# Attention and a routed feed-forward on one core: where the 15 one-tile units stand in the order of 75, and how the last unit is added

## The reference

```
x = x + attention(layernorm(x), ctx, ctx)        # 16 heads of 16, four projections with biases
n = layernorm(x)
p = softmax(n @ router)                          # 8 experts; the best 2 of each token, their
w = softmax(top_2(p))                            # probabilities softmaxed once more
x = x + sum over the 2 experts e: w_e * ((silu(n @ gating_e) * (n @ up_e)) @ down_e)
```

## Time and profile before

| | |
|---|---|
| median of 3 executions | 1276.99 us (1273.31 to 1278.37) |
| the profiled execution: its time | 1274.27 us |
| its span in the trace | 1272.5 us |
| PE busy | 1221.5 us, 96% of the span |
| PE weight loads | 991.1 us, 78% |
| DVE busy | 645.8 us, 51% |
| ACT busy | 561.3 us, 44% |
| POOL busy | 424.4 us, 33% |
| mean granted clock of PE | 0.991 of full speed |

### The profile page before, as it was taken

How to read it: one execution, slowest core, us unless ns; L and a number is a source line. 1 busy time by engine, 2 the same in 40 slices (tenths; PEclk the granted TensorE clock), 3 DMA queues, 4 the chain that set the end, 5 groups by cost and what they waited for, 6 DMA issues and landing times.

```text
span 1272.5 us, 30742 instructions
## 1 busy us (share of the span) xinstructions
PE 1221.5 (96%) x11214; PEld 991.1 (78%) x11215; DVE 645.8 (51%) x1762; ACT 561.3 (44%) x924; POOL 424.4 (33%) x354
## 2 busy tenths in 40 slices
PE   6999999999999999799999999999999999999996
PEld 3677777777767676578887888888888888888996
DVE  3778888888888778623453222332222222232332
ACT  3566666666666665535322222222222322222442
POOL 3211333333333333322464222223332322222322
PEclk9999999999999999899999999999999999999999
DMA  4444455545545332424344333333333433333332
GB/s 130 138 117 122 152 152 149 157 151 154 155 140 151 114 117 82 106 48 67 77 89 71 50 50 50 53 52 53 50 50 50 54 50 52 51 50 43 53 51 33
DMA packets 171586, 112.44 MB, mean 88 GB/s; under 512 B 103345, under 2 KB 158641, under 8 KB 171473
## 3 DMA queue, kind: packets, MB, share of 16 engines
q1 hardware_dynamic: 143984, 72.75, 23.2%
q0 software_dynamic: 26400, 37.09, 16.6%
q10 hardware_dynamic: 1088, 1.05, 0.3%
HBM read 48.59 MB, written 45.46 MB: 74 GB/s over the span
## 4 chain that ended last, share of the span: by engine, by line
PE 89%; DVE 4%; DMA 2%; issue 2%; ACT 1%; SPq 0%; POOL 0%; another core or an unknown queue 0%; ACTq 0%; POOLq 0%; DVEq 0%
PE banks L522 71%; PE banks L551 5%; PE banks L565 4%; PE banks L576 4%; DVE row_max L1028 1%; PE banks L528 1%; PE banks L557 1%; DMA heads<-qT 1%; PE banks L592 1%; DMA out<-x_sb,token 1%; PE banks L600 1%; DVE att_rows L1041 1%; DVE q_less L1035 1%; DMA ctxT_sb<-in_ctx 0%; PE banks L606 0%
## 5 line engine op out<-in xcount | busy, mean ns | idle before, releaser
L481 POOL DMA_INDIRECT out<-x_sb,token x135 | 210.4, 1559 | 478.2 <-DVE x_sb L1346 413.5
L873 ACT ACTIVATE qT<-banks 128x1024 f32<-128x1024 f32 (+1 forms) x75 | 70.4, 939 | 488.6 <-PE banks L522 430.4
L1333 DVE TENSOR_TENSOR heads<-qT,banks 128x1024 f32<-128x1024 f32 (+1 forms) x75 | 83.5, 1113 | 356.7 <-PE banks L522 338.8
L522 PE MATMUL banks<-xnT,probs 128*128 128x256 f32 (+1 forms) x1184 | 242.7, 361 | 4.4 <-issue 4.4
L522 PE MATMUL banks<-down_sb,heads 128*128 x1080 | 245.5, 379 | 1.2 <-DVE x_sb L1346 0.9
L522 PE MATMUL banks<-xnT,kT 128*128 128x256 f32 (+1 forms) x1216 | 244.8, 359 | 0.0
L522 PEld LDWEIGHTS banks<-xnT,probs 128*128 128x128 f32 x1184 | 208.6, 191 | 32.9 <-issue 7.9
L522 PEld LDWEIGHTS banks<-xnT,kT 128*128 128x128 f32 x1216 | 213.1, 192 | 26.6 <-issue 1.0
L522 PEld LDWEIGHTS banks<-down_sb,heads 128*128 128x128 f32 x1080 | 204.0, 190 | 29.2 <-issue 2.2
L434 POOL DMA_INDIRECT sorted_x<-xn,slots_now x128 | 125.2, 978 | 251.5 <-PE banks L551 139.6
L1028 DVE TENSOR_REDUCE row_max<-banks 128x16 f32<-128x2048 f32 x64 | 146.6, 2291 | 64.2 <-PE banks L551 64.1
(11 more groups left out here) (165 smaller groups left out, 1269.2 us busy)
## 6 DMA issues: line engine op xcount, KB each, us to landing
xn<-sorted_x SPq DMA_DIRECT2D x240, 64.0 KB
x_sb<-in_x SPq DMA_DIRECT2D x16, 512.0 KB, 4.0
ctxT_sb<-in_ctx SPq DMA_DIRECT2D x16, 512.0 KB
heads<-kT SPq DMA_DIRECT2D x128, 64.0 KB
heads<-qT SPq DMA_DIRECT2D x128, 64.0 KB
out<-x SPq DMA_DIRECT2D x16, 512.0 KB
gate_sb<-_L_ffn_kernel_gating_EDF SPq DMA_DIRECT2D x8, 512.0 KB
up_sb<-in_L_ffn_kernel_up_EDF SPq DMA_DIRECT2D x8, 512.0 KB
```

Source lines behind the costliest of these rows:

```text
L481: pool.indirect_dma_start(out=out[:, :], out_offset=bass.IndirectOffsetOnAxis(ap=token[:, v, h:h + 1], axis=0), in_=ys[:, 2 * u + h, :], i ...
L522: last = nc.tensor.matmul(dst, lhsT, rhs, start=(i == 0), stop=(i == len(pairs) - 1))
L873: nc.scalar.activation(gatedT[:, 0:w * F], gate_up[:, 0:w * F], ACT.Silu).then_inc(s_silu, 1)
L1333: nc.vector.tensor_tensor(fusedT[:, u, 0:w * F], gatedT[:, 0:w * F], gate_up[:, 1024:1024 + w * F], ALU.mult).then_inc(s_fuse, 1)
```

## The change

The table's order becomes: units 0 to 15 early pairs, 16 to 30 singles, 31 to 74 late pairs. So `wide` and `added` change, `late_table` writes its two parts to other places, and units 1 to 32 are written out (`PEELED` = 8); the loop has 10 rounds and covers units 33 to 72; 73 and 74 are written out behind it. The waits for the finished table and for the stored residuals, which stood ahead of the loop, now stand ahead of unit 13, the same unit as before. SP's loop goes from 22 to 21 rounds of two units. The last unit, now a pair, is treated apart: its two tiles go to two banks, each with a signal of its own, DVE weights them in two instructions with a wait and a signal each, and POOL adds each with a wait of its own.

```diff
@@ -42,10 +42,11 @@
 LATE = PAIRS - EARLY
-PEELED = 3
-ROUNDS = (PAIRS - 1) // 4
-assert 4 * PEELED + 3 < EARLY <= SURE
-assert 32 * PEELED < 128 and TILES % 2 == 1
+PEELED = (EARLY + SINGLES) // 4 + 1
+ROUNDS = (UNITS - 3) // 4
+TABLE_FROM = 13
+assert TABLE_FROM + 2 < EARLY <= SURE
+assert 4 * PEELED > EARLY + SINGLES and TILES % 2 == 1
 
@@ -247,10 +248,10 @@
         def added(n):
-            return 32 * n if not isinstance(n, int) else 32 * min(n, PAIRS) + 16 * max(n - PAIRS, 0)
+            return 32 * n - 16 * SINGLES if not isinstance(n, int) else 32 * n - 16 * min(max(n - EARLY, 0), SINGLES)
 
         def wide(n):
-            return 2 if not isinstance(n, int) or n < PAIRS else 1
+            return 1 if isinstance(n, int) and EARLY <= n < EARLY + SINGLES else 2
 
@@ -371,10 +372,12 @@
             sp.wait_ge(s_pad, EXPERTS * 16)
-            with sp.Fori(EARLY // 2 - 1, PAIRS // 2 - 1) as tt:
+            for n in range(EARLY - 2, 4 * PEELED - 2):
+                next_unit(n, n % 2)
+            with sp.Fori(2 * PEELED - 1, 2 * ROUNDS) as tt:
                 for u in range(2):
                     next_unit(tt * 2 + u, u)
-            for n in range(PAIRS - 2, UNITS - 2):
+            for n in range(4 * ROUNDS, UNITS - 2):
                 next_unit(n, n % 2)
@@ -506,13 +509,22 @@
                 behind_tile(2 * n + 1)
-                add_unit(n, n % 2, n % 4, 2)
-            pool.wait_ge(s_res, GROUPS * 16)
+                if n == TABLE_FROM:
+                    pool.wait_ge(s_res, GROUPS * 16)
+                add_unit(n, n % 2, n % 4, wide(n))
             with pool.Fori(PEELED, ROUNDS) as tt:
...
                     add_unit(tt * 4 + v + 1, (v + 1) % 2, (v + 1) % 4, 2)
-            for n in range(4 * ROUNDS + 1, UNITS):
-                add_unit(n, n % 2, n % 4, wide(n))
+            for n in range(4 * ROUNDS + 1, UNITS - 1):
+                add_unit(n, n % 2, n % 4, 2)
+            for h in range(2):
+                pool.wait_ge(s_y, UNITS + h)
+                if h == 0:
+                    pool.wait_ge(s_acc, added(UNITS - 1))
+                pool.nop(nofuse=True)
+                pool.indirect_dma_start(
+                    out=out[:, :], out_offset=bass.IndirectOffsetOnAxis(ap=token[:, (UNITS - 1) % 4, h:h + 1], axis=0),
+                    in_=ys[:, 2 * ((UNITS - 1) % 2) + h, :], in_offset=None, compute_op=ALU.add).then_inc(s_acc, 16)
             pool.wait_ge(s_acc, added(UNITS))
@@ -735,10 +747,13 @@
                 wait(pe, s_y, n)
+                ends_stage = isinstance(n, int) and n == UNITS - 1
                 for h in range(w):
-                    last = product(work[:, 0, h * D:(h + 1) * D],
-                                   [(fusedT[:, u, (c * w + h) * P:(c * w + h + 1) * P], down_sb[:, bass.ds(e * (FC * D) + c * D, D)])
-                                    for c in range(FC)])
+                    y = work[:, h, 0:D] if ends_stage else work[:, 0, h * D:(h + 1) * D]
+                    last = product(y, [(fusedT[:, u, (c * w + h) * P:(c * w + h + 1) * P],
+                                        down_sb[:, bass.ds(e * (FC * D) + c * D, D)]) for c in range(FC)])
+                    if ends_stage and h == 0:
+                        last.then_inc(s_down, 1)
                 last.then_inc(s_down, 1)
@@ -790,14 +805,15 @@
             for n in range(1, 4 * PEELED + 1):
-                unit(n, n % 2, 2)
-            pe.wait_ge(s_table, TABLE_STEPS)
+                if n == TABLE_FROM:
+                    pe.wait_ge(s_table, TABLE_STEPS)
+                unit(n, n % 2, wide(n))
             with pe.Fori(PEELED, ROUNDS) as tt:
...
                 unit(n, n % 2, wide(n))
-            down_(UNITS - 1, (UNITS - 1) % 2, 1)
+            down_(UNITS - 1, (UNITS - 1) % 2, 2)
 
@@ -977,8 +993,9 @@
             for n in range(1, 4 * PEELED + 1):
-                unit(n, n % 2, 2)
-            act.wait_ge(s_table, TABLE_STEPS)
+                if n == TABLE_FROM:
+                    act.wait_ge(s_table, TABLE_STEPS)
+                unit(n, n % 2, wide(n))
             with act.Fori(PEELED, ROUNDS) as tt:
@@ -1159,7 +1176,7 @@
                 steps.then(nc.vector.tensor_copy(row_table[:, first:first + n], row_f[0:1, 0:n]))
-                if first == PAIRS:
+                if first == EARLY:
                     steps.then(nc.vector.tensor_scalar(expert_f[:, 0:n], expert_f[:, 0:n], float(EXPERTS - 1), None, ALU.min))
@@ -1224,7 +1241,7 @@
                     steps.then(nc.vector.tensor_scalar(row_f[:, 0:LATE], row_f[:, 0:LATE], done[:, 0:1], None, ALU.add))
-                    write_table(steps, EARLY, LATE, 2 * P)
+                    write_table(steps, EARLY + SINGLES, LATE, 2 * P)
                     steps.then(nc.vector.tensor_tensor(paired[:], paired[:], done[:], ALU.add))
@@ -1239,7 +1256,7 @@
                     steps.then(nc.vector.tensor_scalar(row_f[:, 0:SINGLES], row_f[:, 0:SINGLES], paired[:, 0:1], None, ALU.add))
-                    write_table(steps, PAIRS, SINGLES, P)
+                    write_table(steps, EARLY, SINGLES, P)
                     assert steps.base + steps.n == TABLE_STEPS, (steps.base, steps.n)
@@ -1413,14 +1430,17 @@
             for n in range(1, 4 * PEELED + 1):
-                unit(n, n % 2, n % 4, 2, (n + 1) // 2 + 1)
+                unit(n, n % 2, n % 4, wide(n), (n + 1) // 2 + 1)
             with dve.Fori(PEELED, ROUNDS) as tt:
...
             dve.wait_ge(s_acc, added(UNITS - 2))
-            copy_y(UNITS - 1, (UNITS - 1) % 2, (UNITS - 1) % 4, 1)
+            for h in range(2):
+                dve.wait_ge(s_down, UNITS + h)
+                nc.vector.tensor_scalar(ys[:, 2 * ((UNITS - 1) % 2) + h, :], work[:, h, 0:D], weight[:, (UNITS - 1) % 4, h:h + 1],
+                                        None, ALU.mult).then_inc(s_y, 1)
```

## The result

The changed kernel takes 1279.85 us (median of 15 executions, 1276.35 to 1285.76), the kernel before 1276.47 (15 executions beside them). The ratio is 1.0026, with a 95% interval of 1.0014 to 1.0038: slower by 3.3 us, within 1.8 and 4.9.

A forecast was written before the change was run, and what follows sets the result against it. PE was taken to bound stage B and POOL's landing adds the tail. Body 0 plus end +2.4 gave 1276.7 us on the profiled execution; with the four executions' mean as base, the forecast was 1278.1 us, range 1273.5 to 1284.0.

The forecast's parts named there:

- The body costs nothing: Stage B: same 15 singles at 5.30 us and 60 pairs at 10.36, borders and written-out units free; 0 us.
- The rival of stops in the longer straight stretch: Units 13 to 32, written out, meet PE stops like unit 11's 6.9 us: +9.3 us, 1285.0 us; chance 0.12.
- A turn of the loop costs a stop: Rival: the loop's 11th turn goes and its stop with it, faster, 1269.3 us or less; chance 0.04.
- The end sets the time: Tail on POOL: unit 73's two adds must land before unit 74's, so the last add starts 2.39 us later.
- Step 2: End: unit 73, now a pair, starts its adds at T + 1.92 and T + 3.77, T being its down's end on PE.
- Steps 3 and 4: End: unit 73's second add lands after 3.77 us, unit 74's first starts 0.75 us later, its second 1.85 behind.
- the term: The end's delay of the last add's start: +2.4 us, between +2.2 and +2.9.
- The two banks and the single copies are worth nothing: Unit 74's results, ready near T + 3.8 and T + 5.5, hide behind unit 73's adds; 0 us.
- the signs of being wrong: PE stops with no releaser in units 13 to 32, or a last add before 1267 us without them.
- the sum: The profiled execution's 1274.27 us plus 2.4 for the end: 1276.7 us for its twin.

The follow-up runs named there:

- the written-out kernel: The kernel before, its order of units kept, with units 1 to 32 written out and the loop from 33 to 56: 0.9992 of the kernel before.
- the early down: The changed kernel with the down of unit 73 and its copy put ahead of unit 74's up product and fuse: 0.9998 of the kernel before.
- the seven kernels with this end: Changed kernel (timed twice), and with one bank, shorter POOL loop, two plain transfers, 24 nops or two indirect transfers more: 1.0020 to 1.0043 of the kernel before.

## Why the prediction was right, and where it was off

- **The body costs nothing**: right. Singles at 5.30 us, pairs at 10.36, both borders without a gap, the 0.0 us between unit 12 and T, and the written-out kernel at 0.9992. The rival of stops in the longer straight stretch did not come. The stops of unit 11 stay where they were and differ by chip: they are in 6 of the 14 traces and absent in the 8 of two other chips, in changed kernels as in others.
- **A turn of the loop costs a stop** had 4 in 100. No trace shows one; written out, five turns fewer gave 0.9992 with 1.0001 as the upper end. In the trace of before no instruction queue moves a packet from 800 to 1147 us, all of it inside the loop, so the turns fetched nothing. The Trainium skill ("Runtime: NRT & Kernel Launch", section "Instruction fetch mechanics") has a taken branch wait for a fetch only when its target is out of the buffered pages. The trace agrees as far as it goes: nothing was fetched and no turn waited. The prediction was wrong to read the rule as a price on each turn of this loop.
- **The end sets the time**, by unit 73's two adds and their landing: right, and shown from both sides by the early down, which took the last add 3.5 us nearer to PE's last products and brought the ratio from 1.0033 to 0.9998.
- **Its size was off.** Step 2 put unit 73's first add at T + 1.92, by a pair 17 units before the end; it came at T + 3.33. Steps 3 and 4 held: 4.45 us from the second add to the next unit's first (4.52 was predicted), 1.87 us between two adds (1.85). With step 2 as measured the term is +3.8 us, not +2.4, outside my +2.2 to +2.9. The interval of the changed kernel's ratio holds both (+2.4 us would be 1.0019); the traces tell them apart, and so do four of the seven kernels with this end, whose intervals lie above 1.0019. That the median of 1279.85 us fell inside the range of 1273.5 to 1284.0 is no test of this term: the range is far wider than the 1.4 us in question. The row that would have told me, unit 71's late add at 1251.95, was in the trace of before, where the singles absorb it. The prediction doesn't mention it and doesn't ask what stands fourth from the last in the changed order.
- **The two banks and the single copies are worth nothing**: right, and for the reason given. The results were ready at T + 4.00 and T + 5.65, for the 3.8 and 5.5 of the prediction, and neither set anything. They are worth 0.85 us where unit 73 lands sooner.
- Of the signs of being wrong neither came: there are no stops in units 13 to 32, and the last add is not before 1267 us but at 1271.86, in an execution that was 2.4 us later at T than the sum had it.

## What to carry to other kernels

Where transfers at the end must land one behind the other, the tail is a chain of its own: cost it from the start of each add to the landing of the last, for the last three or four units and not only the last. Small units at the end let such a chain catch up while the bound engine is still at work; large ones leave it whole behind the last product. And splitting a result into parts pays only when nothing else holds up what it feeds until the whole result would have been ready. Here the landing did; with one down moved in front of one up it ended sooner, and then the split was worth something.

## What was not expected of the hardware

- The fourth indirect transfer from GpSimd's last starts late in every trace: 1.3 to 1.4 us when it had to wait anyway, 2.35 us between two adds of a pair (2.65 for 0.30). It didn't move with the loop, with more transfers ahead of it or with nops behind it. What it is stays open.
- TensorE's stops in units 7 and 11 went with the chip in these runs, not with the kernel. Counted from the end of the down ahead of it, unit 11 takes 17.4 and 18.5 us in the traces of before and after, and 10.36 us (658.05 to 668.41) in the changed kernel on another chip. PE's timeline there:

```profile
654.60 3.62 PE L534 MATMUL banks<-down_sb,heads 128*128 x16
658.05 7.07 PE L534 MATMUL banks<-xnT,probs 128*128 128x256 f32 x32
...
668.41 7.07 PE L534 MATMUL banks<-xnT,kT 128*128 128x256 f32 x32
```
